# Row factors of three blocks through DRAM, and the high parts of the summed weights streamed beside the low ones

## The reference, cut to what matters

```
scale = cond @ norm_w.T + 1.0
h  = x * (scale[:, None, :] * rsqrt(mean(x * x, axis=-1) + EPS))
u  = h @ up_w.T                       # 512 -> 4096, split in val and gate
h  = val * gelu(gate, approximate=False)
hq = round(h * 127 / max|h| of the row), clipped, times max|h| / 127
y  = hq @ ternary(down_w).T           # 2048 -> 512
return y + x
```

## Time and profile before

| | us |
|---|---|
| median of 3 runs | 759.24 (759.22 to 759.32) |
| the profiled execution | 759.19 |
| its span, first to last instruction | 757.4 |
| around the span | 1.8 |
| PE busy | 737.0 (97%) |
| DVE busy | 546.7 (72%) |
| ACT busy | 345.7 (46%) |
| POOL busy | 98.9 (13%) |

### The profile page before, as it was taken

One profiled execution on the slowest core, in us unless ns is written; L12 is line 12 of the kernel. 1 busy time (PEld: TensorE's weight loads), 2 busy tenths in 40 slices (PEclk: granted clock), 3 DMA queues, 4 the chain that ended last, 5 costly groups with the idle time before them and its releaser, 6 DMA issues.

```text
span 757.4 us, 15715 instructions
## 1 busy us (share of the span) xinstructions
PE 737.0 (97%) x6218; PEld 610.5 (81%) x6218; DVE 546.7 (72%) x1066; ACT 345.7 (46%) x674; POOL 98.9 (13%) x137
## 2 busy tenths in 40 slices
PE   3999999999999999999999999999999999999998
PEld 2888889888578887888778887788878887688864
DVE  5467777888788775878667775777758776377747
ACT  5789756443254432553235442444325342233425
POOL 2211376763413000000000000000000000000000
PEclk9999999999999999999999999999999999999999
DMA  9877673756645444343533434343443333453302
GB/s 324 285 259 241 189 264 123 229 178 223 200 135 183 153 153 148 116 140 99 183 117 116 130 116 163 108 152 122 125 160 103 98 98 117 128 170 98 103 29 84
DMA packets 43929, 116.63 MB, mean 154 GB/s; under 512 B 4944, under 2 KB 5200, under 8 KB 42704
## 3 DMA queue, kind: packets, MB, share of 16 engines
q1 hardware_dynamic: 43856, 115.63, 47.6%
HBM read 98.83 MB, written 16.78 MB: 153 GB/s over the span
## 4 chain that ended last, share of the span: by engine, by line
PE 86%; DVE 5%; ACT 3%; issue 3%; DMA 1%; POOL 0%; SPq 0%; DVEq 0%; ACTq 0%
PE ps_v L525 16%; PE ps_v L526 15%; PE ps_v L527 15%; PE ps_y L626 12%; PE ps_g L526 8%; PE ps_g L525 8%; PE ps_g L527 8%; PE ps_v L690 1%; DMA sums<-in_up_t_dram 1%; DMA h<-in_x_rows_dram 1%; ACT g L733 1%; ACT w_hi L776 1%; DVE h L1053 0%; PE ps_m L609 0%; DVE xt L1004 0%
## 5 line engine op out<-in xcount | busy, mean ns | idle before, releaser
L525 PE MATMUL ps_v<-x_hi,w_hi 128*128 128x256 f16 x1216 | 332.0, 273 | 3.3 <-DVE ps_g L1036 1.3
L527 PE MATMUL ps_v<-x_hi,w_lo 128*128 128x256 f16 x1216 | 331.9, 273 | 0.0
L526 PE MATMUL ps_v<-x_lo,w_hi 128*128 128x256 f16 x1216 | 331.9, 273 | 0.0
L526 PE MATMUL ps_g<-x_lo,w_hi 128*128 128x256 f16 x640 | 174.8, 273 | 0.0
L527 PE MATMUL ps_g<-x_hi,w_lo 128*128 128x256 f16 x640 | 174.8, 273 | 0.0
L525 PE MATMUL ps_g<-x_hi,w_hi 128*128 128x256 f16 x640 | 174.8, 273 | 0.0
L715 ACT COPY ps_g<-ps_v 128x256 f32<-128x256 f32 x96 | 34.3, 357 | 230.7 <-PE ps_v L527 230.7
L525 PEld LDWEIGHTS ps_v<-x_hi,w_hi 128*128 128x128 f16 x1216 | 119.1, 98 | 21.4 <-DVE ps_g L1036 2.7
L526 PEld LDWEIGHTS ps_v<-x_lo,w_hi 128*128 128x128 f16 x1216 | 119.1, 98 | 15.7
L527 PEld LDWEIGHTS ps_v<-x_hi,w_lo 128*128 128x128 f16 x1216 | 119.1, 98 | 13.9
L726 ACT ACTIVATE g<-ps_g,w_unscale 128x512 f32<-128x512 f32 x128 | 87.3, 682 | 68.1 <-PE ps_g L527 68.0
(11 more groups left out here) (113 smaller groups left out, 581.7 us busy)
## 6 DMA issues: line engine op xcount, KB each, us to landing
w_lo<-w_lo_dram SPq DMA_DIRECT2D x96, 448.0 KB, 3.3
q<-in_up_t_dram SPq DMA_DIRECT2D x16, 512.0 KB, 5.1
xt<-in_x_cols_dram SPq DMA_DIRECT2D x8, 1024.0 KB, 5.2
res<-in_x_rows_dram SPq DMA_DIRECT2D x26, 256.0 KB, 3.6
out_dram<-res SPq DMA_DIRECT2D x26, 256.0 KB, 2.9
sums<-in_up_t_dram SPq DMA_DIRECT2D x12, 512.0 KB, 4.7
xs<-in_x_rows_dram SPq DMA_DIRECT2D x22, 256.0 KB, 3.8
w_lo_dram<-w_lo SPq DMA_DIRECT2D x16, 256.0 KB, 4.8
```

The lines of the kernel that those rows point to most:

```text
L525: pe.matmul(to, w_hi[:, wh:wh + P], hi, start=start and kt == 0, stop=False, skip_group_check=True)
L526: pe.matmul(to, w_hi[:, wh:wh + P], lo, start=False, stop=False, skip_group_check=True)
L527: last = pe.matmul(to, w_lo[:, wl:wl + P], hi, start=False, stop=(kt == 1), skip_group_check=True)
```

## The change

Three edits. For blocks 5, 6 and 7 (`RS_DRAM = 5`) the row factors are stored to DRAM at j = 13 of block c - 2 and loaded at j = 14, broadcast to all partitions, into the first half of `xs`; ACT puts them in column order into the second half at j = 15, and `norm` reads them there and no longer in `ps_m`. `spread_rs` runs for blocks 0 to 4 alone. Second, the high parts of the four sums are written by ACT beside the low parts and stored and loaded with them, so that a slot of `w_lo` grows from 2048 to 3072 columns, a load from step 32 on from 3584 to 5632 bytes of each partition, and a store of the sums from 2048 to 4096 bytes. Third, with that the layout of the raw weights of the sums and several waits change their place.

```
     WJ = 2 * KT * P
-    WO = NOP * 2 * P
     WA = 4 * 2 * P
     WS = 4 * 2 * P
-    WL = WA + WS
+    WL = WA + 2 * WS
     PAD = 2 * P
...
+
+    RS_DRAM = 5
+
...
+        rs_dram = nc.dram_tensor("rs_dram", [NB, P * TT], F32, kind="Internal").ap()
         lo_dram = nc.dram_tensor("w_lo_dram", [J, P, WL], FP16, kind="Internal").ap()
...
-
-        w_hi = sb("w_hi", [P, PAD + J * WO], FP16)
+        w_hi = sb("w_hi", [P, J * WA], FP16)
         w_lo = sb("w_lo", [P, LS * WL], FP16)
...
         xs = sb("xs", [P, 2, D], F32)
+        sum_out = sb("sum_out", [P, 2 * WS], FP16)
         res = sb("res", [P, 2, D], F32)
...
         rs_rows = sem("rs_rows")
+        rs_stored = sem("rs_stored")
+        rs_loaded = sem("rs_loaded")
         xn_ready = sem("xn_ready")
...
-            return PAD + j * WO
+            return j * WA + PAD
...
             if place < 2:
-                return sums[:, place * WS:(place + 1) * WS].rearrange("p (a n) -> p a n", a=2)
-            slots = w_lo[:].bitcast(F32).rearrange("p (s c) -> p s c", s=LS)
-            return slots[:, 2 * place - 4:2 * place - 2, WA // 2:WL // 2]
+                return sums[:, place * WS:(place + 1) * WS]
+            return w_lo[:, place * WL + WA:(place + 1) * WL].bitcast(F32)
...
-            return xs[:, k % 2, :].bitcast(FP16)
+            return sum_out[:] if k % 2 == 0 else xs[:].rearrange("p a n -> p (a n)").bitcast(FP16)
...
                     sp.wait_ge(dw_ready, J)
-                sp.dma_start(sum_raw(k), up_t[k].rearrange("p (a n) -> p a n", a=2)).then_inc(sum_loaded[SUM_PLACE[k]], 16)
+                sp.dma_start(sum_raw(k), up_t[k]).then_inc(sum_loaded[SUM_PLACE[k]], 16)
...
                     if n < 2 * J + LS:
-                        last = max(k for k in range(J) if SUM_PLACE[k] == 2 + (n % LS) // 2)
-                        sp.wait_ge(ws_ready, last + 1)
+                        if n % LS in (2, 3):
+                            sp.wait_ge(ws_ready, max(k for k in range(J) if SUM_PLACE[k] == n % LS) + 1)
                     if n < 3 * J:
...
                     sp.wait_ge(sumsq_ready, TT + t + 1)
+                if c > RS_DRAM and i < 2:
+                    sp.wait_ge(xn_ready, c * KT)
                 if c == 4 and i < 2:
-                    stored, count = sum_store(J - 2 + t % 2)
+                    stored, count = sum_store(J - 1)
                     sp.wait_ge(stored, count)
...
+
+            def store_rs(c):
+                sp.wait_ge(rs_ready, c + 1)
+                sp.dma_start(rs_dram[c].rearrange("(p i) -> p i", p=P), rs[:]).then_inc(rs_stored, 16)
+
+            def load_rs(c):
+                sp.wait_ge(rs_stored, 16 * (c - RS_DRAM + 1))
+                sp.dma_start(xs[:, 0, :], rs_dram[c].unsqueeze(0).to_broadcast([P, P * TT])).then_inc(rs_loaded, 16)
...
                             load_xs(c, i)
+                for c in range(RS_DRAM, NB):
+                    if n == rsqrt_at(c) + 2:
+                        store_rs(c)
+                    if n == rsqrt_at(c) + 3:
+                        load_rs(c)
                 if b >= 1 and j in (14, 15):
...
                 for kt in range(2):
-                    wh = wb(j) + (op * 2 + kt) * P
                     wl = (n % LS) * WL + PAD + (op * 2 + kt) * P
+                    if op >= OS3:
+                        w = w_lo[:, wl + WS:wl + WS + P]
+                    else:
+                        wh = wb(j) + (op * 2 + kt) * P
+                        w = w_hi[:, wh:wh + P]
                     xa = x_at(b, xop) + kt * HB
                     hi, lo = x_hi[:, xa:xa + HB], x_lo[:, xa:xa + HB]
-                    pe.matmul(to, w_hi[:, wh:wh + P], hi, start=start and kt == 0, stop=False, skip_group_check=True)
-                    pe.matmul(to, w_hi[:, wh:wh + P], lo, start=False, stop=False, skip_group_check=True)
+                    pe.matmul(to, w, hi, start=start and kt == 0, stop=False, skip_group_check=True)
+                    pe.matmul(to, w, lo, start=False, stop=False, skip_group_check=True)
                     last = pe.matmul(to, w_lo[:, wl:wl + P], hi, start=False, stop=(kt == 1), skip_group_check=True)
...
                 pe.wait_ge(lo_loaded[n % LS], 16 * ((n - J) // LS + 1))
-                if n < 3 * J:
-                    pe.wait_ge(ws_ready, n % J + 1)
                 if n >= NV:
...
                 pe.wait_ge(h_max_ready, (b + 1) * J)
-                pe.wait_ge(xn_ready, min(b + 3, NB) * KT)
+                pe.wait_ge(xn_ready, min(b + 3, RS_DRAM) * KT)
                 pe.wait_ge(scaled_ready, b * J)
...
                     spread_scale(b - 1)
-                for c in range(1, NB):
+                for c in range(1, RS_DRAM):
                     if n == spread_rs_at(c):
...
+            def order_rs(c):
+                act.wait_ge(rs_loaded, 16 * (c - RS_DRAM + 1))
+                act.copy(xs[:, 1, :].rearrange("p (i q) -> p i q", i=TT),
+                         xs[:, 0, :].rearrange("p (q i) -> p i q", i=TT)).then_inc(rs_rows, 1)
+
...
                 act.wait_ge(s_step, 4 * (k + 1))
-                act.wait_ge(val_ready, J + min(k + 2, J))
-                act.activation(w_hi[:, wb(k) + WA - PAD:wb(k) + WO].rearrange("p (a n) -> p a n", a=2), sum_raw(k), ACT.Copy,
+                if k >= 2:
+                    stored, count = sum_store(k - 2)
+                    act.wait_ge(stored, count)
+                if k == 1:
+                    act.wait_ge(sumsq_ready, 3 * TT)
+                act.activation(sum_tile(k)[:, WS:2 * WS], sum_raw(k), ACT.Copy,
                                scale=w_scale[:, k:k + 1]).then_inc(ws_hi_ready, 1)
...
                             square(c, i)
+                for c in range(RS_DRAM, NB):
+                    if n == rsqrt_at(c) + 4:
+                        order_rs(c)
                 if 2 <= n < 2 + ND:
...
             def sum_weights(k):
-                a21, a22, a11, a12 = [sum_raw(k)[:, i // 2, (i % 2) * 2 * P:(i % 2 + 1) * 2 * P] for i in range(4)]
+                a21, a22, a11, a12 = [sum_raw(k)[:, i * 2 * P:(i + 1) * 2 * P] for i in range(4)]
                 pool.wait_ge(sum_loaded[SUM_PLACE[k]], sum_loads(k) * 16)
...
                 dve.wait_ge(ws_hi_ready, k + 1)
-                dve.wait_ge(sumsq_ready, 3 * TT)
-                if k >= 2:
-                    stored, count = sum_store(k - 2)
-                    dve.wait_ge(stored, count)
-                dve.scalar_tensor_tensor(out=sum_tile(k).rearrange("p (a n) -> p a n", a=2), in0=sum_raw(k),
-                                         scalar=w_scale[:, k:k + 1],
-                                         in1=w_hi[:, wb(k) + WA - PAD:wb(k) + WO].rearrange("p (a n) -> p a n", a=2),
+                dve.scalar_tensor_tensor(out=sum_tile(k)[:, 0:WS], in0=sum_raw(k), scalar=w_scale[:, k:k + 1],
+                                         in1=sum_tile(k)[:, WS:2 * WS],
                                          op0=ALU.mult, op1=ALU.subtract).then_inc(ws_ready, 1)
...
                 at = kt * B + c // PER_B
-                dve.scalar_tensor_tensor(out=xt[:, kt, :], in0=xt[:, kt, :], scalar=cs[:, at:at + 1], in1=ps_m[:],
+                rows = ps_m[:] if c < RS_DRAM else xs[:, 1, :]
+                dve.scalar_tensor_tensor(out=xt[:, kt, :], in0=xt[:, kt, :], scalar=cs[:, at:at + 1], in1=rows,
                                          op0=ALU.mult, op1=ALU.mult).then_inc(xn_ready, 1)
```

## The result

The changed kernel takes 761.80 us in the median of 7 runs (759.82 to 764.32), the kernel before 759.32 in 7 runs on the same chip (759.13 to 760.01). The ratio is 1.0036, 95% interval 1.0022 to 1.0049: it is slower by 0.36%, where 759.1 us and no difference were forecast, and the median lies above the range of 757.5 to 760.9. The change has also made the time less even: 4.5 us between the fastest and the slowest run against 0.9. The kernel before is not always as even as in these seven runs, though.

A forecast was written before the change was run, and what follows sets the result against it. PE was taken as the bound, busy 737.0 of 757.4 us. From 759.19 us: -1.32 for the spreads, +1.41 for group 14's burst, -0.2 at 208.7 us, giving 759.1 us; range 757.5 to 760.9.

The forecast's parts named there:

- the spreads: Blocks 4, 5, 6 on PE: three spreads of four transposes removed, 0.44 us each, 1.32 us gained in all.
- Store, load and ACT's copy: New row-factor path through DRAM: store, broadcast load and ACT copy all in time, cost 0.
- C: Rival: DVE holds PE at later waits, so the spreads' time is given back; 760.4 us, chance 0.09.
- group 14: Burst ahead of its raw weights' load: 524 KB more delay the landing and PE by 1.41 us.
- the 2.5 that the prediction had named as a sign of being wrong: Landing of group 14's raw weights: growth by over 2.5 us, or none, would show the prediction wrong.
- the stall of 0.86 becomes about 2.3, that of 0.45 stays: PE's stalls at 236.9 and 239.4 us: the whole 1.41 us delay arrives at the first, none at the second.
- Rival B: Group 14's sums much later: added bytes take 1.88 us and POOL's work is stretched by 1.4; 761.2 us, chance 0.14.
- The neighbours have room: Groups 13 and 15: POOL's results ready 2.8 and 1.2 us before ACT takes them; both cost 0.
- fits: ACT's moved wait for a store, tightest at the fifth high part: 6.55 us available, by more than 1 us enough.
- the small gain at 208.7: PE's stall before the transposes of the maxima: POOL starts later, DVE's low part runs quicker, 0.2 us gained.
- the steady blocks: Larger loads of 704 KB land in 4.2 us, issued over 9 us before use; nothing reaches PE, cost 0.

The follow-up runs named there:

- the half alone: Kernel before with only the row factors of blocks 5 to 7 sent through DRAM, larger sums transfers left out: 758.40 us, ratio 0.9982.
- the early groups: Raw weights of groups 14 and 15 requested one step earlier: ratio 0.9990 on the kernel before, 0.9974 with row factors through DRAM and no larger sums transfers.
- the sixth experiment: Kernel before with the raw weights of group 14 requested one step later, no larger transfers: 763.87 us, ratio 1.0047.
- loads first and early groups: Changed kernel, raw weights' load issued ahead of the sums' store within a step, groups 14 and 15 requested one step earlier: 758.11 us, ratio 0.9981.
- the one with both groups early: Changed kernel with the raw weights of groups 14 and 15 requested one step earlier: 758.66 us, ratio 0.9988.
- the run before it: Changed kernel with the raw weights of group 14 alone requested one step earlier: 759.13 us, ratio 0.9994.
- loads first: Changed kernel with the raw weights' load issued ahead of the store of sums within a step: 760.46 us, ratio 1.0009.
- the stream alone: Changed kernel with RS_DRAM = 8: sums' high parts stored and loaded with the low ones, all eight spreads kept on PE: 763.26 us, ratio 1.0046.

## Why the prediction was wrong

**Right: the spreads.** The windows are shorter by 0.44 or 0.45 us each, and the half alone gained 1.0 us. With the early groups the kernel with and without spreads stands at 0.9974 and 0.9990, again 1.2 us apart. Store, load and ACT's copy ended no wait of PE. C, in which DVE gives that time back, did not happen.

**Right in kind and nearly in size: group 14.** The forecast had the landing from 5.5 to 6.9 us and the stalls from 1.31 to 2.7. The landing took 8.3, 7.4 and 7.4 us in three profiles with the larger transfers, and the stalls were 2.95, 2.43 and 2.93 us. The burst is under-sized (1.9 to 2.8 us more in place of 1.41), and in the profiled execution the growth of 2.8 us is above the 2.5 that the prediction had named as a sign of being wrong. A part of this did not reach PE, as POOL's four took 3.2 us in place of 3.5. The Trainium skill's figure ("DMA: Bandwidth & Descriptors", the anatomy of one DMA), an estimate of 1.20 us for the added bytes, is further off than the rate read from the burst; the measurement decides. That fit is stated for single DMAs that GpSimd issues, and here SP has several under way.

**The step that failed** is "the stall of 0.86 becomes about 2.3, that of 0.45 stays", taken as the price of the delay. A stall of PE was counted at its length. In ten of 19 runs it costs about 3 us more, since the clock falls with it. No row of the kernel before shows it; its stalls there are short, and made longer in the sixth experiment they bring it to that kernel in six of ten runs. With that clock the median is 763.6, without it 760.5, which is inside the range of 757.5 to 760.9. Since about half of the runs are hit, the median over all falls between the two groups, and where exactly (761.8, then 762.3) is partly chance. Rival B had the sign and nearly the time (761.2), but for the reason that POOL's work is stretched, which did not happen: POOL was quicker.

**The second step that failed** is the term of all the other groups, put at nothing: the prediction looked at the neighbours 13 and 15 ("The neighbours have room", "Both cost 0"), and for these it held in the changed kernel as it stands. The early groups were looked at only for ACT's moved wait, which "fits", and with a store of 4.8 us (4.0 and 0.8), where the first larger store took 7.2. The tightest case was the third high part, that of group 2, and not the fifth: in the changed kernel it began 0.4 us after that store had landed, and with loads first and early groups ACT stood 0.9 us for it. Group 3's raw weights stand behind the first larger store: they landed in 8.0 us in place of 7.0, in a stretch in which the chain runs over DVE. (Landings of 7.9 to 8.0 in three of the other profiles with the old order, 5.7 in the one with both groups early, whose load went out 2.2 us later than in the run before it.) PE's stall at 180 us was 0.76, 1.53, 1.39, 2.40 and 0.74 us in the profiles with the stream and requests in the old order, 0.37 and 0.36 with loads first, and 0 to 0.59 without the stream. The landing is not all of it: the one with 2.40 us had its group 3 landed at 141.0 us, where the one with 1.39 us had it at 141.1. How POOL's work falls on DVE's instructions differs as well (the low part takes 1.28 to 1.79 us), and I have not separated the two. In the runs of 0.999 and more these terms add up: -1.3 for the spreads, +1.4 at 239, +0.8 to 1.5 at 180 are +0.9 to 1.6, against 760.5 - 759.3 = 1.2 measured. The four runs of the stream alone with a full clock do not fit this sum by over 1 us.

**Met, but by luck as far as the runs tell: the small gain at 208.7.** The low part took 1.28 us and the stall went to 1.05, a gain of 0.27 where 0.2 was taken. The reason given was that the larger transfers hold POOL back. But the row factors alone, without larger transfers, have the same 1.28 and 1.05 us, though POOL's instruction runs beside the low part and takes 1.71 us there. And the changed kernel with loads first and early groups has 1.63 and 1.40. So the gain comes and goes with how the low part and POOL's instructions meet, which differs between executions. The stall with the row factors alone, and the one with loads first and early groups:

```profile
209.48 0.63 PE L629 MATMUL ps_m<-ident,h_max 128*128 128x128 f32 x4 [1.05 <-issue]
...
210.26 0.63 PE L632 MATMUL ps_m<-ident,h_max 128*128 128x128 f32 x4 [1.40 <-issue]
```

**Right, and without effect: the steady blocks.** 704 KB land in 4.3 us in the median, 6.3 at most, and PE never waits for them.

## What to carry to other kernels

A stall of the bounding engine is not to be priced at its length alone: look whether a longer one lowers its clock, and give such a case its own place in the range. Before a transfer is made larger, look for the request behind it in the same queue that an idle engine is already waiting for, and ask for that one a step earlier; here this is worth about 1 us in the kernel before and over 3 us in the changed one. When one exposed chain is mended, compute the next one anew, since its room was measured while the first held everything up.

## What the runs showed of the hardware

ACT's reordering copy of 128 x 512 with a stride of four elements on the reading side took 1.11 us, where a plain activation of that size takes 0.63 to 0.69 (no plain copy of that size ran, so the stride's own share is not shown):

```profile
373.56 0.69 ACT L748 ACTIVATE g<-ps_g,w_unscale 128x512 f32<-128x512 f32 x1 [0.79 <-PE ps_g L551]
374.15 1.11 ACT L778 COPY xs<-xs 128x512 f32<-128x512 f32 x1
```

The store of 128 rows of 16 bytes, 2 KB in all, needed 3.8 us to land each of three times. The broadcast load of 256 KB took 5.6 in the median of three (4.5 to 5.7), against 4.4 for 16 plain loads of that size into the same tile (3.5 to 6.2), all from 250 us on:

```profile
xs<-in_x_rows_dram SPq DMA_DIRECT2D x16, 256.0 KB, 4.4
...
xs<-rs_dram SPq DMA_DIRECT2D x3, 256.0 KB, 5.6
...
rs_dram<-rs SPq DMA_DIRECT2D x3, 2.0 KB, 3.8
```

TensorE's clock went to its lower level (1.2 GHz) with two stalls close together of 2.7 us (1.67 and 1.05) and 2.95 us (1.90 and 1.05) in two profiles. In two others it stayed up with three stalls of 2.93 and 2.43 us in the same place, as it did in all ten runs of the kernel with loads first, whose profile has 2.32 us. Which of two like executions is hit was not to be told from the profiles.
